# A graph transformer layer: three heads for each squaring instruction, from three PSUM banks, in place of two heads from two

## The chip, the cores and the metric

The kernel runs on one core of a Trainium2 chip. The metric is the device time of one execution in microseconds (us). Before the change it is 252.06 us, the median of three runs (251.73 to 252.9).

## The reference, cut to what matters

A layer over 625 nodes of 256 features: layer norm, then a graph step (mean of the neighbours' rows, two linear maps) and an attention step side by side, both added to x; then layer norm, and a feed forward net of 1024 hidden units whose output projection is that of one of eight experts for each node. The part that matters here is the attention, with 8 heads of 32 dimensions. Its weights are a second order expansion of exp, so that it has no maximum and no exponential:

```python
qn = _normalize(q) * (scale * temperature)
kn = _normalize(k) * scale
vN = v1 / N                      # v1 is v with a column of ones ahead
kv_mod = jnp.einsum('bhni,bhnj,bhne->bhije', kn, kn, vN)
kv = jnp.einsum('bhnd,bhne->bhde', kn, vN)
vsum = jnp.sum(vN, axis=-2)[:, :, None, :]
y = A * jnp.einsum('bhni,bhnj,bhije->bhne', qn, qn, kv_mod) \
    + scale ** 2 * Bc * jnp.einsum('bhnd,bhde->bhne', qn, kv) + scale ** 4 * Cc * vsum
y = y[..., 1:] / y[..., :1]      # A = 0.5, Bc = Cc = 1
```

For one query and one key with the product s the weight is s*s/2 + c*s + c*c (c is a constant). The kernel computes it as the square of (s + c) plus c*c, up to a factor that the division removes: so each score is computed once, squared with a bias, and multiplied by v.

## The kernel before, in words

All five engines run programs written out by hand, with semaphores between them; nothing is planned by a compiler. The order of the work on an engine is the order of its source. In order of time: the layer norm and the projections; the neighbour counts, built as products of one-hot rows (up to about 92 us of the profile); **the attention (93.6 to 126.9 us)**; transposes of the count matrix (L1146); the projections and the sum over neighbours (L1165 to L1176); the first layer of the feed forward net, its gate, the sorting of nodes by expert, the first layer again on sorted rows (L1260), the experts (L1276).

The attention computes, for a group hg of four heads (two groups), one half hf of the queries (313 or 312 of them) and one tile m of 125 keys (five tiles), two products for each head h:

- the scores (`scores`, L1085 to L1100): keys by queries, a matmul with 32 rows of the array (tile_position `(D * h, 0)`) and 125 columns, into a PSUM bank of its own;
- the values (`values`, L1103 to L1121): the squares times v, a matmul with all 125 rows and 32 columns of the array (tile_position `(0, D * h)`), accumulated over the five tiles m into 32 partitions of bank 6 or 7.

That makes 2 x 2 x 5 x 4 = 80 heads' worth of work, written as 160 matmul instructions at each of the two lines, since an fp32 product is issued as two instructions. Between the two products ScalarE squares: the source has 40 `units` (L386), each with two heads, whose scores lie in two neighbouring banks and are squared by one instruction (L622, 125 partitions x 626 elements) into one of `NGB = 4` buffers of `gsq`. `gsq` lies in `qk_sb`, where the rows of q and k were. Three pairs of banks, 0 to 5, go round (`SLOTS = 3`).

TensorE's program takes four heads at a time (two units, the index u2): `scores(u2 + 1)`, then `values(u2)`, twenty times. Its waits: `scores` waits, before each pair of heads, until the unit that used this pair of banks three units earlier is squared (L1094); `values` waits until both of its units are squared (L1107). ScalarE waits for the scores of its unit (L618) and, from the fifth unit on, until the buffer of squares is read (L620). VectorE leads each finished half out of bank 6 or 7 (L820, L823). Ahead of the loop TensorE waits until the banks of the neighbour counts are copied out by ScalarE (banks 0 and 2, L613) and VectorE (the others, L801), and fills the wait with `kept_busy` matmuls on zeros (L1083). Once, at u2 == 2, it adds up v (L1136).

Of the kernel before, what the change touches and what calls it, by code (L numbers as in the profile page):

```python
# [11 lines left out]
ACT = mybir.ActivationFunctionType  # L12
AX = mybir.AxisListType

P = 128
# [4 lines left out]
def gps_layer(nc, x, edges, w_qkv, b_qk, b_v, w_lr, b_r, w_proj, b_proj, temp,  # L20
              w1, b1, wg, bg, wd, bd, rows_sorted, out):
    N, C = out.shape
    TP = 125
    T = N // TP
# [8 lines left out]
    D = C // H  # L33
    HG = P // D
# [5 lines left out]
    HALF = [(0, (N + 1) // 2), ((N + 1) // 2, N)]  # L40
    HW = HALF[0][1]
# [7 lines left out]
    with ExitStack() as ctx:  # L49
# [6 lines left out]
        ps = ctx.enter_context(nc.psum_tensor("ps", [P, 8, BANK], F32))  # L56
# [30 lines left out]
        big = mem[:, WD:WD + BIG]  # L87
# [5 lines left out]
        sc2_col = sb("sc2_col", [P, 1])  # L93
# [22 lines left out]
        qk_sb = sb("qk_sb", [P, T * 4 * QB])  # L116
# [8 lines left out]
        qT = qkT[:, 0:2 * N].rearrange("p (k n) -> p k n", k=2)  # L125
        kT = qkT[:, 2 * N:4 * N].rearrange("p (k n) -> p k n", k=2)
# [22 lines left out]
        v = vz[:, :, 0:C]  # L149
# [6 lines left out]
        bd_all = vz_flat[:, 0:E * C]  # L156
        v_sum = row[:, 0, 0:C]
        NGB = 4
        gsq = qk_sb[0:TP, 0:NGB * 2 * HW].rearrange("p (b i n) -> p b i n", b=NGB, i=2)
        yT_sb = sb("yT_sb", [P, T * 2 * (P + 1)])  # L160
        yT = yT_sb[:, 0:2 * N].rearrange("p (k n) -> p k n", k=2)
        uq = yT
# [85 lines left out]
        A_copied_a = sem("A_copied_a")  # L248
        A_copied_v = sem("A_copied_v")
# [23 lines left out]
        s_ps = sem("s_ps")  # L273
        g_ready = sem("g_ready")
        g_used = sem("g_used")
# [38 lines left out]
        ACT_SUMS = (0, 2)  # L314
# [68 lines left out]
        FIRST_PARTS = ((0, KH // 2), (KH // 2, KH - 1), (KH - 1, KH))  # L383


        units = [(hg, hf, m, pr) for hg in range(2) for hf in range(2) for m in range(T) for pr in range(2)]  # L386
        SLOTS = 3
        LN_PARTS = ((0, 2), (2, T))

        block = ctx.enter_context(nc.Block())  # L390
# [124 lines left out]
        def _(act):  # L515
# [27 lines left out]
            for k in range(1, T):  # L543
                ins = nc.scalar.activation(ge[:, k - 1].rearrange("p g j -> p (g j)"), dst_f[:, :], ACT.Sign,
                                           bias=below[:, k - 1:k], scale=2.0)
# [57 lines left out]
            for j, (hg, hf) in enumerate(halves):  # L603
                lo, hi = HALF[hf]
# [7 lines left out]
                if n in ACT_SUMS:  # L612
                    nc.scalar.copy(sums, banks).then_inc(A_copied_a, 1)  # L613

            for u, (hg, hf, m, pr) in enumerate(units):
                lo, hi = HALF[hf]
                w = hi - lo
                act.wait_ge(s_ps, u + 1)  # L618
                if u >= NGB:
                    act.wait_ge(g_used, (u - NGB) // 2 + 1)  # L620
                b = 2 * (u % SLOTS)
                nc.scalar.activation(gsq[:, u % NGB, :, 0:w], ps[0:TP, b:b + 2, 0:w], ACT.Square,  # L622
                                     bias=sc2_col[0:TP, :]).then_inc(g_ready, 1)

            for n, (counts, blocks) in enumerate(at_parts()):
                if n in ACT_AT:
# [20 lines left out]
            for part in range(2):  # L647
                lo, hi = columns(part)
# [25 lines left out]
        def _(dve):  # L674
# [106 lines left out]
            for hg in range(2):  # L781
                nc.vector.tensor_tensor(MA[:, hg, :], ps[:, 7, QB * hg:QB * hg + P], blk[:, :], ALU.mult)
                ins = nc.vector.tensor_scalar(ks[:, hg:hg + 1], ps[:, 7, QB * hg + P:QB * (hg + 1)], 2 * SC2, None,
                                              ALU.mult)
# [4 lines left out]
            for j, (hg, hf) in enumerate(halves):  # L789
                lo, hi = HALF[hf]  # L790
# [25 lines left out]
            dve.wait_ge(v_sum_read, 1)  # L816
            for k in range(4):
                hg, (lo, hi) = k // 2, HALF[k % 2]
                dve.wait_ge(g_used, T * (k + 1))
                nc.vector.scalar_tensor_tensor(yT[:, hg, lo:hi], ps[:, 6 + k % 2, 0:hi - lo], vs[:, hg:hg + 1],  # L820
                                               rn[:, hg, lo:hi], ALU.add, ALU.mult).then_inc(y_left, 1)
                dve.wait_ge(y_left, k + 1)
                nc.vector.tensor_scalar(yT[:, hg, lo:hi], yT[:, hg, lo:hi], bv_sb[:, hg:hg + 1], None, ALU.add  # L823
                                        ).then_inc(y_ready, 1)
                if k == 0:
                    step(nc.vector.reciprocal(rn[:, 1, :], rn[:, 1, :]))
# [7 lines left out]
            for t in range(T):  # L834
                a, rest = (ps[0:TP, b, :] for b in RP_BANKS[t % 2])
# [24 lines left out]
            for part, tiles in enumerate(TOKENS):  # L860
                lo, hi = columns(part)
                own, NT = slice(tiles[0], tiles[-1] + 1), len(tiles)
# [79 lines left out]
        def _(pe):  # L942
            mm = nc.tensor.matmul
# [122 lines left out]
            for j, (hg, hf) in enumerate(halves):  # L1066
                lo, hi = HALF[hf]
# [3 lines left out]
            for j, (hg, hf) in enumerate(halves):  # L1071
                lo, hi = HALF[hf]
# [8 lines left out]
            def kept_busy(n, b):  # L1081
                for _ in range(n):
                    mm(ps[:, b, :], zeros[:, 0:P], zeros[:, :], start=True, stop=True)  # L1083

            def scores(u2):  # L1085
                hg, hf, m, _ = units[2 * u2]
                lo, hi = HALF[hf]
                for h in range(HG):
                    u = 2 * u2 + h // 2
                    if h % 2 == 0 and u < SLOTS:  # L1090
                        pe.wait_ge(A_copied_a, (1, 2, 2)[u])
                        pe.wait_ge(A_copied_v, (1, 2, 4)[u])
                    if h % 2 == 0 and u >= SLOTS:
                        pe.wait_ge(g_ready, u + 1 - SLOTS)  # L1094
                    rows = slice(D * h, D * (h + 1))
                    ins = mm(ps[0:TP, 2 * ((2 * u2 + h // 2) % SLOTS) + h % 2, 0:hi - lo],  # L1096
                             kT[rows, hg, TP * m:TP * (m + 1)], qT[rows, hg, lo:hi], start=True, stop=True,
                             tile_position=(D * h, 0))
                    if h % 2:
                        ins.then_inc(s_ps, 1)  # L1100


            def values(u2):  # L1103
                hg, hf, m, _ = units[2 * u2]
                lo, hi = HALF[hf]
                k = 2 * hg + hf
                pe.wait_ge(g_ready, 2 * u2 + 2)  # L1107
                if u2 == 0:
                    pe.wait_ge(A_copied_v, 5)
                if k == 1 and m == 0:  # L1110
                    pe.wait_ge(v_sum_read, 1)
                if m == 0 and k >= 2:
                    pe.wait_ge(y_left, k - 1)
                for pr in range(2):
                    for i in range(2):
                        h = 2 * pr + i
                        ins = mm(ps[D * h:D * (h + 1), 6 + k % 2, 0:hi - lo],  # L1117
                                 v[:, m, P * hg + D * h:P * hg + D * (h + 1)],
                                 gsq[:, (2 * u2 + pr) % NGB, i, 0:hi - lo], start=(m == 0), stop=(m == T - 1),
                                 tile_position=(0, D * h), skip_group_check=True)  # L1120
                ins.then_inc(g_used, 1)  # L1121

            U2 = len(units) // 2
            pe.wait_ge(b7_free, JOBS)
            kept_busy(3, 7)
            scores(0)
            kept_busy(2, 7)
            for u2 in range(U2):
                if u2 + 1 < U2:
                    scores(u2 + 1)  # L1130
                if u2 == 0:
                    kept_busy(2, 7)
                if u2 == 2:
                    pe.wait_ge(v_tiles, 1)
                    for hg in range(2):
                        ins = mm(ps[:, 7, C + hg:C + hg + 1], v_sum[:, P * hg:P * (hg + 1)], ones_c[0:TP, 0:1],  # L1136
                                 start=True, stop=True)
                    ins.then_inc(v_sum_ps, 1)
                values(u2)

            pe.wait_ge(g_ready, len(units))
            pe.wait_ge(A_ready, T)
# [183 lines left out]
```

## Time and profile before

| | |
|---|---|
| median of three runs | 252.06 us |
| the profiled execution | 251.73 us |
| its span, first to last instruction | 250.0 us |
| mean granted TensorE clock | 0.997 of full speed |
| TensorE matmuls busy | 235.7 us, 94% of the span |
| VectorE busy | 148.2 us, 59% |
| ScalarE busy | 145.2 us, 58% |
| attention, first scores to first transpose | 93.6 to 126.9 us |

All times come from one profiled execution. A busy share is an average over stages with different limits; the chain of waits says which engine set the time of a stretch. Matmuls that run at the same time in different parts of the array are shown as one merged row with a count ("x8"), whose second number is the length from the first start to the last end.

### The profile page before, as it was taken

The numbers are of one execution on the slowest core, as the hardware profiler recorded it, in microseconds if no ns is written. First come the engines' busy times: TensorE is split into PE (matmuls) and PEld (weight loads), VectorE is DVE, ScalarE is ACT, GpSimd is POOL, SyncE is SP. The second block draws the span as 40 slices with busy tenths as digits, with TensorE's granted clock in tenths as the row PEclk, the third lists the DMA queues.
The fourth block names the chain that finished last, engine by engine and source line by source line (L and its number), as shares of the span: only waits on it lengthen the run. The fifth ranks groups of instructions, "written<-read, shape, count | busy, mean of one in ns | idle before, by whom it ended". The sixth has DMA issues, their size and how long they took to land.

```text
span 250.0 us, 4726 instructions
## 1 busy us (share of the span) xinstructions
PE 235.7 (94%) x1428; PEld 149.4 (60%) x1429; DVE 148.2 (59%) x422; ACT 145.2 (58%) x223; POOL 31.7 (13%) x64
## 2 busy tenths in 40 slices
PE   7899999999897999999999999998899999999990
PEld 2448676655454553433378886564455578888880
DVE  2999999999999969950134649523700243223320
ACT  3977998999999967899950116443043332333000
POOL 7460000000000019100000000000540000000331
PEclk9999999999999999999999999999999999999998
DMA  6560000000000000199910000030123000000111
GB/s 233 194 215 3 1 3 5 3 4 5 0 5 3 3 3 3 37 413 425 416 59 4 0 0 0 24 134 9 32 79 106 0 1 3 0 1 3 38 34 33
DMA packets 6030, 15.82 MB, mean 63 GB/s; under 512 B 2724, under 2 KB 3783, under 8 KB 4723
## 3 DMA queue, kind: packets, MB, share of 16 engines
q1 hardware_dynamic: 4432, 12.64, 13.6%
q0 software_dynamic: 1280, 1.31, 2.0%
q10 hardware_dynamic: 288, 1.44, 1.4%
q8 instruction: 21, 0.34, 0.6%
q14 instruction: 9, 0.07, 0.1%
HBM read 14.08 MB, written 1.30 MB: 62 GB/s over the span
## 4 chain that ended last, share of the span: by engine, by line
PE 69%; DVE 26%; ACT 1%; issue 1%; POOL 1%; DVEq 0%; POOLq 0%
PE ps L1276 17%; DVE mem L728 14%; PE ps L1214 7%; PE ps L1096 7%; PE ps L1260 6%; DVE mem L731 6%; PE ps L1117 5%; PE ps L1176 4%; PE ps L1010 4%; PE ps L1244 3%; PE ps L945 3%; PE ps L1165 2%; PE ps L1167 2%; PE ps L973 1%; DVE qk_sb L774 1%
## 5 line engine op out<-in xcount | busy, mean ns | idle before, releaser
L523 ACT ACTIVATE mem<-ids_m,half_src 125x628 bf16<-125x628 f16 x96 | 69.8, 815 | 0.0
L1010 PE MATMUL ps<-mem 125*128 125x501 bf16 x180 | 51.3, 374 | 2.2 <-issue 2.0
L728 DVE TENSOR_SCALAR mem<-node_ids,dst_f 125x628 bf16<-125x628 f16 x160 | 52.1, 371 | 0.0
L1276 PE MATMUL ps<-mem 128*125 x192 | 41.6, 379 | 0.0
L1012 PE MATMUL ps<-mem 125*128 125x126 bf16 x180 | 39.3, 219 | 0.0
L1276 PEld LDWEIGHTS ps<-mem 128*125 128x125 f32 x192 | 36.0, 188 | 5.4
L1010 PEld LDWEIGHTS ps<-mem 125*128 x180 | 17.6, 98 | 22.5 <-issue 4.8
L622 ACT ACTIVATE qk_sb<-ps,sc_col 125x626 f32<-125x626 f32 (+1 forms) x40 | 28.6, 779 | 3.7 <-PE ps L1096 3.7
L731 DVE TENSOR_SCALAR mem<-ids_m,src_f 125x628 bf16<-125x628 f16 x64 | 23.9, 374 | 0.0
L671 ACT COPY mem<-mem 128x1000 f32 x8 | 8.2, 1031 | 19.8 <-PE ps L1276 19.8
L1096 PE MATMUL ps<-mem 32*125 32x313 f32 (+1 forms) x160 | 19.1, 472 | 0.2 <-DVE mem L801 0.2
L1012 PEld LDWEIGHTS ps<-mem 125*128 x180 | 17.5, 97 | 2.3 <-issue 1.2
L1214 PE MATMUL ps<-xnT,w_sb 128*128 128x375 f32 (+1 forms) x64 | 18.4, 432 | 0.0
L935 DVE SCALAR_TENSOR_TENSOR row<-vz,row x12 | 5.8, 485 | 20.1 <-issue 20.1
L920 DVE COPY mem<-mem 128x500 f32 (+2 forms) x12 | 4.1, 393 | 20.3 <-ACT mem L663 20.0
L505 POOL DMA_INDIRECT rows_sorted<-row,pos x5 | 6.2, 1236 | 77.3 <-DVE pos L893 76.1
L1260 PE MATMUL ps<-xnT,w_sb 128*128 128x512 f32 (+1 forms) x56 | 15.3, 433 | 0.0
L1117 PE MATMUL ps<-qk_sb,vz 125*32 125x313 f32 (+1 forms) x160 | 14.7, 439 | 0.6 <-ACT qk_sb L622 0.6
L1096 PEld LDWEIGHTS ps<-mem 32*125 32x125 f32 x160 | 8.9, 180 | 10.5 <-issue 5.0
L1214 PEld LDWEIGHTS ps<-xnT,w_sb 128*128 128x128 f32 x64 | 11.6, 189 | 5.5 <-ACT mem L651 1.2
L973 PE MATMUL ps<-wqkv_sb,xnT 128*125 128x512 f32 (+1 forms) x40 | 14.1, 487 | 0.8 <-ACT xnT L551 0.8
L651 ACT ACTIVATE mem<-ps,b_sb 128x375 f32<-128x375 f32 (+1 forms) x16 | 8.3, 522 | 9.4 <-PE ps L1214 9.4
(204 smaller groups left out, 280.0 us busy)
## 6 DMA issues: line engine op xcount, KB each, us to landing
mem<-in_wd SPq DMA_DIRECT2D x8, 1024.0 KB, 13.1
w_sb<-in_w SPq DMA_DIRECT2D x1, 1024.0 KB, 8.2
vz<-in_bd SPq DMA_DIRECT2D x1, 1000.0 KB
wqkv_sb<-in_w_qkv ACTq DMA_DIRECT2D x1, 768.0 KB, 6.1
x_all<-in_x ACTq DMA_DIRECT2D x1, 640.0 KB, 4.7
row<-rows_sorted SPq DMA_DIRECT2D x1, 579.7 KB
wlr_sb<-in_w_lr SPq DMA_DIRECT2D x1, 512.0 KB, 5.5
bqk_all<-in_b_qk SPq DMA_DIRECT2D x1, 256.0 KB, 4.7
```

What stands on the lines that cost most here:

```text
L523: ins = nc.scalar.activation(oh[:, g % OHB, 0, j, :], ids_m1[:, :], ACT.Sign, bias=half_src[:, g * GC + j:g * GC + j + 1])
L622: nc.scalar.activation(gsq[:, u % NGB, :, 0:w], ps[0:TP, b:b + 2, 0:w], ACT.Square, bias=sc2_col[0:TP, :]).then_inc(g_ready, 1)
L728: ins = nc.vector.tensor_scalar(oh[:, g % OHB, 1, j, :], node_ids[:, :], dst_f[:, col:col + 1], None, ALU.is_equal)
L731: ins = nc.vector.tensor_scalar(oh[:, g % OHB, 0, j, :], ids_m1[:, :], src_f[:, col:col + 1], 2.0, ALU.is_ge, ALU.mult)
L973: ins = mm(ps[0:TP, QKV_BANKS[n], lo:hi], xnT[:, c, TP * t:TP * (t + 1)], w[:, c, :], start=(c == 0), stop=(c == KC - 1))
L1010: mm(psf[:, bass.ds(tile * BANK, TW + 1)], node_of, oh[:, buf, 0, j, 0:TW + 1], start=False, stop=False, skip_group_check=True)
L1012: mm(psf[:, bass.ds(tile * P + 5 * BANK, AW)], node_of, oh[:, buf, 0, j, TW:N + 1], start=False, stop=False, skip_group_check=True)
L1096: ins = mm(ps[0:TP, 2 * ((2 * u2 + h // 2) % SLOTS) + h % 2, 0:hi - lo], kT[rows, hg, TP * m:TP * (m + 1)], qT[rows, hg, lo:hi], start=Tru ...
L1117: ins = mm(ps[D * h:D * (h + 1), 6 + k % 2, 0:hi - lo], v[:, m, P * hg + D * h:P * hg + D * (h + 1)], gsq[:, (2 * u2 + pr) % NGB, i, 0:hi ...
L1214: ins = mm(fa_bank(part, k), w1_sb[:, c, P * k:P * (k + 1)], x2nT[:, c, lo:hi], start=(c == 0), stop=(c == KC - 1))
L1260: ins = mm(psf[:, at + lo:at + hi], w1_sb[:, c, P * k:P * (k + 1)], x2nT[:, c, lo:hi], start=(c == 0), stop=(c == KC - 1))
L1276: ins = mm(ps[0:TP, 4 + n % EB, 0:C], hT_step[:, n % EB, k, :], wd_sb[:, bass.ds(e, 1), k, :], start=(k == 0), stop=(k == KH - 1))
```

## The change

A unit now holds up to three heads (`UH = 3`). For each of the four combinations of group and half, the 20 pairs (m, h) are listed in order and cut into 6 units of three and one of two: 28 units in all instead of 40, each squared by one instruction from up to three neighbouring banks. There are two slots of three banks (0 to 2, 3 to 5). TensorE's loop goes over units instead of pairs of units: `scores(u + 2)`, then `values(u)`, 28 times, with one more `scores(1)` ahead of it. A unit may hold heads of two key tiles. `scores` waits once, ahead of its first head, for the unit two earlier; `values` waits for its own unit. The buffers of squares are four of 3 x 313 elements, in `big` (where the one-hot rows of the counts were), instead of four of 2 x 313 in `qk_sb`. The wait for the count banks is put ahead of each head of the first two units.

```diff
@@ -156,7 +156,8 @@
         bd_all = vz_flat[:, 0:E * C]
         v_sum = row[:, 0, 0:C]
         NGB = 4
-        gsq = qk_sb[0:TP, 0:NGB * 2 * HW].rearrange("p (b i n) -> p b i n", b=NGB, i=2)
+        UH = 3
+        gsq = big[0:TP, 0:NGB * UH * HW].rearrange("p (b i n) -> p b i n", b=NGB, i=UH)
         yT_sb = sb("yT_sb", [P, T * 2 * (P + 1)])
         yT = yT_sb[:, 0:2 * N].rearrange("p (k n) -> p k n", k=2)
         uq = yT
@@ -383,8 +384,10 @@
         FIRST_PARTS = ((0, KH // 2), (KH // 2, KH - 1), (KH - 1, KH))
 
 
-        units = [(hg, hf, m, pr) for hg in range(2) for hf in range(2) for m in range(T) for pr in range(2)]
-        SLOTS = 3
+        heads = [(m, h) for m in range(T) for h in range(HG)]
+        units = [(k, heads[n:n + UH]) for k in range(4) for n in range(0, len(heads), UH)]
+        PER_K = len(units) // 4
+        SLOTS = 2
         LN_PARTS = ((0, 2), (2, T))
 
         block = ctx.enter_context(nc.Block())
@@ -612,15 +615,14 @@
                 if n in ACT_SUMS:
                     nc.scalar.copy(sums, banks).then_inc(A_copied_a, 1)
 
-            for u, (hg, hf, m, pr) in enumerate(units):
-                lo, hi = HALF[hf]
-                w = hi - lo
+            for u, (k, own) in enumerate(units):
+                lo, hi = HALF[k % 2]
                 act.wait_ge(s_ps, u + 1)
                 if u >= NGB:
-                    act.wait_ge(g_used, (u - NGB) // 2 + 1)
-                b = 2 * (u % SLOTS)
-                nc.scalar.activation(gsq[:, u % NGB, :, 0:w], ps[0:TP, b:b + 2, 0:w], ACT.Square,
-                                     bias=sc2_col[0:TP, :]).then_inc(g_ready, 1)
+                    act.wait_ge(g_used, u - NGB + 1)
+                b = UH * (u % SLOTS)
+                nc.scalar.activation(gsq[:, u % NGB, 0:len(own), 0:hi - lo], ps[0:TP, b:b + len(own), 0:hi - lo],
+                                     ACT.Square, bias=sc2_col[0:TP, :]).then_inc(g_ready, 1)
 
             for n, (counts, blocks) in enumerate(at_parts()):
                 if n in ACT_AT:
@@ -816,7 +818,7 @@
             dve.wait_ge(v_sum_read, 1)
             for k in range(4):
                 hg, (lo, hi) = k // 2, HALF[k % 2]
-                dve.wait_ge(g_used, T * (k + 1))
+                dve.wait_ge(g_used, PER_K * (k + 1))
                 nc.vector.scalar_tensor_tensor(yT[:, hg, lo:hi], ps[:, 6 + k % 2, 0:hi - lo], vs[:, hg:hg + 1],
                                                rn[:, hg, lo:hi], ALU.add, ALU.mult).then_inc(y_left, 1)
                 dve.wait_ge(y_left, k + 1)
@@ -1082,61 +1084,58 @@
                 for _ in range(n):
                     mm(ps[:, b, :], zeros[:, 0:P], zeros[:, :], start=True, stop=True)
 
-            def scores(u2):
-                hg, hf, m, _ = units[2 * u2]
-                lo, hi = HALF[hf]
-                for h in range(HG):
-                    u = 2 * u2 + h // 2
-                    if h % 2 == 0 and u < SLOTS:
-                        pe.wait_ge(A_copied_a, (1, 2, 2)[u])
-                        pe.wait_ge(A_copied_v, (1, 2, 4)[u])
-                    if h % 2 == 0 and u >= SLOTS:
-                        pe.wait_ge(g_ready, u + 1 - SLOTS)
+            def bank_left(b):
+                if b in ACT_SUMS:
+                    pe.wait_ge(A_copied_a, 1 + ACT_SUMS.index(b))
+                else:
+                    pe.wait_ge(A_copied_v, b + 1 - sum(a < b for a in ACT_SUMS))
+
+            def scores(u):
+                k, own = units[u]
+                hg, (lo, hi) = k // 2, HALF[k % 2]
+                if u >= SLOTS:
+                    pe.wait_ge(g_ready, u + 1 - SLOTS)
+                for i, (m, h) in enumerate(own):
+                    b = UH * (u % SLOTS) + i
+                    if u < SLOTS:
+                        bank_left(b)
                     rows = slice(D * h, D * (h + 1))
-                    ins = mm(ps[0:TP, 2 * ((2 * u2 + h // 2) % SLOTS) + h % 2, 0:hi - lo],
-                             kT[rows, hg, TP * m:TP * (m + 1)], qT[rows, hg, lo:hi], start=True, stop=True,
-                             tile_position=(D * h, 0))
-                    if h % 2:
-                        ins.then_inc(s_ps, 1)
-
-
-            def values(u2):
-                hg, hf, m, _ = units[2 * u2]
-                lo, hi = HALF[hf]
-                k = 2 * hg + hf
-                pe.wait_ge(g_ready, 2 * u2 + 2)
-                if u2 == 0:
-                    pe.wait_ge(A_copied_v, 5)
-                if k == 1 and m == 0:
+                    ins = mm(ps[0:TP, b, 0:hi - lo], kT[rows, hg, TP * m:TP * (m + 1)], qT[rows, hg, lo:hi],
+                             start=True, stop=True, tile_position=(D * h, 0))
+                ins.then_inc(s_ps, 1)
+
+            def values(u):
+                k, own = units[u]
+                hg, (lo, hi) = k // 2, HALF[k % 2]
+                pe.wait_ge(g_ready, u + 1)
+                if u == 0:
+                    bank_left(6)
+                if u == PER_K:
                     pe.wait_ge(v_sum_read, 1)
-                if m == 0 and k >= 2:
+                if u % PER_K == 0 and k >= 2:
                     pe.wait_ge(y_left, k - 1)
-                for pr in range(2):
-                    for i in range(2):
-                        h = 2 * pr + i
-                        ins = mm(ps[D * h:D * (h + 1), 6 + k % 2, 0:hi - lo],
-                                 v[:, m, P * hg + D * h:P * hg + D * (h + 1)],
-                                 gsq[:, (2 * u2 + pr) % NGB, i, 0:hi - lo], start=(m == 0), stop=(m == T - 1),
-                                 tile_position=(0, D * h), skip_group_check=True)
+                for i, (m, h) in enumerate(own):
+                    ins = mm(ps[D * h:D * (h + 1), 6 + k % 2, 0:hi - lo], v[:, m, P * hg + D * h:P * hg + D * (h + 1)],
+                             gsq[:, u % NGB, i, 0:hi - lo], start=(m == 0), stop=(m == T - 1),
+                             tile_position=(0, D * h), skip_group_check=True)
                 ins.then_inc(g_used, 1)
 
-            U2 = len(units) // 2
             pe.wait_ge(b7_free, JOBS)
             kept_busy(3, 7)
             scores(0)
             kept_busy(2, 7)
-            for u2 in range(U2):
-                if u2 + 1 < U2:
-                    scores(u2 + 1)
-                if u2 == 0:
-                    kept_busy(2, 7)
-                if u2 == 2:
+            scores(1)
+            kept_busy(2, 7)
+            for u in range(len(units)):
+                if u + SLOTS < len(units):
+                    scores(u + SLOTS)
+                if u == 3:
                     pe.wait_ge(v_tiles, 1)
                     for hg in range(2):
                         ins = mm(ps[:, 7, C + hg:C + hg + 1], v_sum[:, P * hg:P * (hg + 1)], ones_c[0:TP, 0:1],
                                  start=True, stop=True)
                     ins.then_inc(v_sum_ps, 1)
-                values(u2)
+                values(u)
 
             pe.wait_ge(g_ready, len(units))
             pe.wait_ge(A_ready, T)
```

## Rows read from the trace of the kernel before

**Rows 1.** The page: busy time of each engine; the chain that ended last.
```profile
PE 235.7 (94%) x1428; PEld 149.4 (60%) x1429; DVE 148.2 (59%) x422; ACT 145.2 (58%) x223; POOL 31.7 (13%) x64
...
PE 69%; DVE 26%; ACT 1%; issue 1%; POOL 1%; DVEq 0%; POOLq 0%
```

**Rows 2.** The chain in order of time: start us, us, what; the attention's start, middle, end.
```profile
94.96 0.54 PE ps L1083 x2
...
109.56 0.66 PE ps L1117 x8
110.22 0.74 PE ps L1096 x8
110.96 0.67 PE ps L1117 x8
111.63 1.00 PE ps L1096 x6
...
126.89 2.92 PE ps L1146 x25
```

**Rows 3.** Groups of instructions by form, 93 to 128 us: busy, mean ns; idle before.
```profile
L622 ACT ACTIVATE qk_sb<-ps,sc_col 125x626 f32<-125x626 f32 x20 | 14.4, 779 | 2.9 <-PE ps L1096 2.9
L622 ACT ACTIVATE qk_sb<-ps,sc_col 125x624 f32<-125x624 f32 x20 | 14.3, 778 | 0.8 <-PE ps L1096 0.8
```

**Rows 4.** Timeline 90 to 104 us, other engines and the sum of v.
```profile
92.75 1.06 ACT L613 COPY mem<-ps 125x501 f32<-125x501 f32 x2 [1.95 <-PE ps L1077]
92.75 2.63 DVE L801 COPY mem<-ps 125x501 f32<-125x501 f32 x5 [2.20 <-PE ps L1077]
94.41 1.46 ACT L622 ACTIVATE qk_sb<-ps,sc_col 125x626 f32<-125x626 f32 x2 [0.60 <-PE ps L1096]
96.70 0.73 PE L1117 MATMUL ps<-qk_sb,vz 125*32 125x313 f32 x8
...
99.77 0.60 PE L1136 MATMUL ps<-ones_c,row 125*128 125x1 f32 x4
100.30 0.16 PEld L1117 LDWEIGHTS ps<-qk_sb,vz 125*32 125x32 f32 x8
```

**Rows 5.** Timeline of narrow windows in the middle: start us, us, instructions merged.
```profile
110.15 0.54 PE L1096 MATMUL ps<-mem 32*125 32x313 f32 x4
...
110.52 0.44 PE L1096 MATMUL ps<-mem 32*125 32x313 f32 x4
110.89 0.73 PE L1117 MATMUL ps<-qk_sb,vz 125*32 125x312 f32 x8
111.56 1.07 PE L1096 MATMUL ps<-mem 32*125 32x313 f32 x8
112.55 0.73 PE L1117 MATMUL ps<-qk_sb,vz 125*32 125x313 f32 x8
```

**Rows 6.** Timeline of narrow windows at the start, TensorE: two heads by themselves.
```profile
93.58 0.53 PE L1096 MATMUL ps<-mem 32*125 32x313 f32 x2 [0.20 <-DVE mem L801]
...
93.92 0.46 PE L1096 MATMUL ps<-mem 32*125 32x313 f32 x2
...
94.17 0.53 PE L1096 MATMUL ps<-mem 32*125 32x313 f32 x2
...
94.50 0.46 PE L1096 MATMUL ps<-mem 32*125 32x313 f32 x2
94.89 0.60 PE L1083 MATMUL ps<-zeros 125*128 125x512 bf16 x2
95.43 0.81 PE L1096 MATMUL ps<-mem 32*125 32x313 f32 x8
96.17 0.60 PE L1083 MATMUL ps<-zeros 125*128 125x512 bf16 x2
```

**Rows 7.** Groups of ScalarE over the span, by form: activations from PSUM of three sizes.
```profile
L663 ACT ACTIVATE mem<-ps,b_sb 128x625 f32<-128x625 f32 x8 | 6.3, 782 | 9.9 <-PE ps L1260 9.7 <-PE ps L1255 0.2
L651 ACT ACTIVATE mem<-ps,b_sb 128x375 f32<-128x375 f32 x8 | 4.5, 574 | 4.1 <-PE ps L1214 4.1
L651 ACT ACTIVATE mem<-ps,b_sb 128x250 f32<-128x250 f32 x8 | 3.8, 470 | 5.3 <-PE ps L1214 5.3
```

**Rows 8.** Timeline 121 to 129 us: the end of the attention.
```profile
124.80 0.73 PE L1117 MATMUL ps<-qk_sb,vz 125*32 125x312 f32 x8
126.15 0.73 PE L1117 MATMUL ps<-qk_sb,vz 125*32 125x312 f32 x8 [0.61 <-ACT qk_sb L622]
126.81 2.37 PEld L1146 LDWEIGHTS ps<-ident,at_sb 125*125 125x125 f32 x21 [0.51 <-issue]
```

## The prediction, written before the change was run

> **What bounds the kernel now.** I read the page first: TensorE is busy 94% of the span, ScalarE 58%, and 69% of the chain that ended last is TensorE's [rows 1]. For the attention this average says little, so I read the chain there in order of time. Without a break it consists of score blocks (L1096) and value blocks (L1117) of TensorE, in a pattern of four that repeats: 0.66, 0.74, 0.67, 1.00 us [rows 2]. That is 3.07 us for two steps of four heads, about 1.53 us each. The groups by form show the other side: 40 squarings of 779 and 778 ns, busy for 28.7 us together, with 3.7 us idle, all of it waiting for TensorE's scores [rows 3]. Two squarings without a wait last 1.46 us [rows 4], so the second starts 1.46 - 0.78 = 0.68 us after the first: ScalarE needs 4 x 0.68 = 2.72 us of each 3.07. So both engines are nearly full, and the reader should ask what each would need alone.
>
> TensorE alone: the timeline of the middle shows a score block from 110.15 and the value block behind it from 110.89, then the next scores at 111.56: 0.74 + 0.67, taken together 1.40 [rows 5]. The block that starts at 111.56 takes until 112.55, 0.99 us: the row of the chain is the long one. There the second pair of heads had to wait for ScalarE. So ScalarE costs TensorE some 0.26 us in every second step, and TensorE alone would need 2.80 of the 3.07 us. This is all that a better ScalarE side can give back: 0.13 us a step, 20 steps, 2.7 us.
>
> **What a block costs.** In rows 5 the first instructions of four heads start together at 110.15, the second ones together at 110.52, and the next block 0.37 us later. A block is thus two waves, and the heads in a wave run side by side, each in its own 32 rows of the array. The question for this change is what a wave with three heads costs. The trace has waves with two: at 93.58 a pair starts, its second wave at 93.92, and the next pair (which waited for a bank) at 94.17, with its second wave at 94.50; the next block of another kind starts at 94.89 [rows 6]. That is 0.34 us from wave to wave, and 94.89 - 94.17 = 0.72 us for a score block of only two heads, against 0.74 with four (95.43 to 96.17, the same neighbour behind it [rows 6]). A wave costs what one head costs; two more heads add 0.02 us. A three-head score block is therefore worth 0.73 us, not three quarters of 0.74. Value blocks with fewer than four heads do not occur; they are waves in the same way (0.67 us with four, [rows 5]), and I take 0.66 for three. Its bounds are 0.50 (in proportion to the heads) and 0.67; I take the upper side, since the score blocks went that way. One step is then 0.73 + 0.66 = 1.39 us.
>
> The Trainium skill has a rule here (TensorE: Matmul & The Clock Gate, section "Why this matters for your kernels"): heads in distinct row groups run concurrently, four tiles reach 3.07 times one tile's rate, three tiles in column groups 2.38 times. An estimate from these two figures: a wave of three costs (3/2.38)/(4/3.07) = 0.97 of a wave of four, so a step costs 0.97 x 1.40 = 1.36 instead of 1.39 and the time would be 0.8 us less than the sum below. The trace's pair (0.72 against 0.74) gives the same 0.97 for two heads already.
>
> **The change, part by part.**
>
> *Fewer, longer squarings.* 24 of 939 elements and 4 of 626. From 375 to 625 elements an activation from PSUM grows from 574 to 782 ns and from 250 to 375 by 104 ns, 0.83 ns per element both times [rows 7]. So 313 more elements make 0.78 + 0.26 = 1.04 us, one each 0.94 us where they follow without a wait. ScalarE's need falls from 40 x 0.68 = 27.2 to 24 x 0.94 + 4 x 0.68 = 25.3 us: 1.9 us, off the path as soon as TensorE needs more. A third bank might cost extra in one instruction; nothing here shows it. The bound is at what point it would matter: scores that start at T have their second wave at T + 0.36, and in the first unit squaring began 94.41 - 93.95 = 0.46 us behind a second wave that started by 93.95 (the pair's second instruction lies 0.03 behind the 93.92 of the row [rows 4, 6]); that makes T + 0.84, squared at T + 1.88, seen by TensorE by T + 1.93. The scores two steps later need it, at T + 2.78. The squaring may be 0.85 us longer before it costs anything.
>
> *28 steps instead of 20.* This is the price. Each step has one score block and one value block, with a change of the array's shape on either side, and three heads in it where there were four (in four of the steps two). The steps' sum grows from 20 x 1.53 = 30.6 to 28 x 1.39 = 38.9 us. Nothing hides it: TensorE is the chain.
>
> *One wait instead of two in a score block.* The wait in mid-block goes with its 0.26 us; it is already in the 1.40. What is late next is TensorE itself.
>
> *The start.* Scores of the first unit need banks 0, 1, 2. ScalarE's second copy (bank 2) ends at 92.75 + 1.06 = 93.81 [rows 4]; the third head starts some 0.15 us later, as the pair did behind VectorE's copy, at 93.96, its second wave at 94.30, the squaring at 94.76 (94.41 before), done at 95.80. Behind the scores two zero matmuls (0.54 from 94.65 [rows 2]); the second unit's scores at 95.19, whose third head needs bank 5: VectorE's five copies end at 92.75 + 2.63 = 95.38, the fourth about 0.2 before, so it starts near 95.34 and the block ends at 96.06; two more zero matmuls, and the loop's first scores start at 96.60. The squares of unit 0 are long there.
>
> *The loop.* Step n starts at 96.60 + 1.39 n, plus 0.53 once for the sum of v (99.77 to 100.30 [rows 4]). Step 25, the last with scores: 96.60 + 34.75 + 0.53 = 131.88. Its scores 0.73: 132.61. Then three value blocks in a row, without scores between them. With the shape unchanged each should take two waves of 0.29 (half of 0.67 less the change of about 0.09), 0.57: 133.18, 133.75, and 134.40 with the change behind the last. The transposes, which started at 126.81 [rows 8], start at 134.40: 7.6 us later.
>
> *The other edits* cost nothing: `gsq` in other memory leaves all instructions as long as they were; its wait counts (four buffers, read one unit at a time) are met two steps ahead; VectorE's four exits at L820 follow TensorE as before, and only the last lies behind the last value block, hidden by 2.92 us of transposes [rows 2] as now. All later work hangs on TensorE's order and moves with it. The loads of the experts' weights, which run under the attention, are not waited for at its end.
>
> **Sum.** 251.73 (the profiled execution: 250.0 of span and 1.7 around it) + 7.6 = 259.3. The median of the runs shown lies 0.3 above the profiled one; I say **259.4 us**.
>
> **The rivals.**
> - *Heads, not waves, set TensorE's price* (the other side). If a block costs in proportion to its heads, a step is 3/4 of 1.40 = 1.05 us. Against the sum: 25 x 0.34 = 8.5 and 0.6 in the last blocks less: 259.4 - 9.1 = 250.3, faster by 1.8. It would decide wherever a step costs less than about 1.39 - 7.6/27 = 1.11 us. For it: only that value blocks with fewer heads are nowhere to be seen. Against: the two-head score blocks [rows 6]. Chance 0.04.
> - *ScalarE is the bound and the change relieves it.* The squarings then run without a gap: from 97.44 (third unit's scores at 96.60 + 0.84) another 25.3 - 1.9 = 23.4 to 120.9, values and change 0.7: 121.6, 5.2 before 126.8, so 246.5. The gaps in ScalarE's row speak for it only in part (3.7 us idle are TensorE's doing [rows 3]). The Trainium skill (TensorEngine Tiling, section "PSUM Bottleneck") says that tiling speeds up TensorE but not the reading of PSUM, which may become the bottleneck, and that one should vectorise PSUM access. The trace does not bear that out here. Chance 0.01.
> - *Part of both*: value blocks in proportion (0.50), score blocks as waves. A step 1.23: 25 x 0.16 + 0.4 = 4.4 less, 255.0. Chance 0.04.
> - *The handshake gets longer*: two slots instead of three. If a three-bank squaring takes over 1.88 us, or the scores wait in mid-block again, a step gains the 0.26 us of the long block: 28 x 0.26 = 7.3, 266.7. Chance 0.03.
> - *The clock*: it is 0.997 on average; TensorE's gaps get shorter, not longer. At half speed the stage would last tens of us more. Chance 0.01.
>
> **How the numbers follow.** The forecast's own case has 0.87: its range, from steps of 1.36 to 1.42 (25 x 0.03 = 0.8) and 0.6 for the runs' scatter, is 258.0 to 260.9; as it holds over 8 in 10, that is the range, with 0.2 more below for value blocks of three that are slightly cheaper: 257.8 to 260.9. A change under 0.5% (1.3 us) can't be told from none. Faster by more: the first two rivals, 0.05. Within: a step between 1.06 and 1.16 us, 0.02. Slower: the rest, 0.93.
>
> **What would show it.** In the changed kernel: the chain of the attention still all TensorE, with blocks near 0.73 (L1096's new line) and 0.66 us, x6 each, none of 1.00; 28 squarings, most near 1.04 us, with gaps of 0.4 us between them; the transposes near 134.4. It is wrong if value or score blocks are near 0.5 us, or if ScalarE's row has no gaps.

## The result: slower by 2.8%

The changed kernel takes 259.31 us (median; 258.94 to 259.31, four runs) against 252.11 us (251.73 to 252.9, four runs, one more than above): a ratio of 1.028, 95% interval 1.026 to 1.030. The forecast was 259.4, the range 257.8 to 260.9. The profiled span is 257.6 us against 250.0.

The page of the changed kernel, busy times and the chain that ended last, answers to [rows 1]:

```profile
PE 243.4 (94%) x1428; PEld 150.4 (58%) x1429; DVE 148.6 (58%) x422; ACT 144.7 (56%) x211; POOL 31.7 (12%) x64
...
PE 66%; DVE 27%; ACT 2%; DMA 2%; issue 1%; POOL 0%; DVEq 0%; ACTq 0%
```

TensorE has the same 1428 matmuls and is busy 7.7 us longer; ScalarE has 12 instructions fewer and is busy 0.5 us less. Neither share of the span says which of the two set the time.

The chain of the changed kernel in order of time (start us, us, what), the middle and the end of the attention, answers to [rows 2]; L1103 are the scores, L1118 the values, L1145 the transposes:

```profile
109.38 0.66 PE ps L1118 x6
110.03 0.73 PE ps L1103 x6
110.76 0.66 PE ps L1118 x6
111.42 0.73 PE ps L1103 x6
112.15 0.66 PE ps L1118 x6
...
132.18 0.72 PE ps L1103 x4
132.90 1.60 PE ps L1118 x16
134.50 2.59 PE ps L1145 x22
```

The long blocks of 1.00 us are gone, as the change means them to be. But the blocks, now with three heads (x6, two instructions a head), last 0.73 and 0.66 us, practically what they lasted with four (0.74 and 0.67, [rows 2]). From 109.38 to 112.15 two steps take 2.77 us, 1.385 each, for three heads a step, six in all; before, two steps took 3.07 us for eight heads.

ScalarE's side, groups by form from 93 to 136 us (count, busy, mean ns, idle before), answers to [rows 3]:

```profile
L624 ACT ACTIVATE mem<-ps,sc_col 125x939 f32<-125x939 f32 x12 | 12.5, 1044 | 4.8 <-PE ps L1103 4.8
L624 ACT ACTIVATE mem<-ps,sc_col 125x936 f32<-125x936 f32 x12 | 12.5, 1042 | 4.7 <-PE ps L1103 4.7
```

A squaring of three banks lasts 1.04 us, as worked out; ScalarE now idles 9.5 us in all ahead of these 24, 0.34 us ahead of most. It was relieved, and nobody needed it. The timeline of the changed kernel shows the same (start, length, idle before):

```profile
109.96 0.80 PE L1103 MATMUL ps<-mem 32*125 32x312 f32 x6
...
110.82 1.04 ACT L624 ACTIVATE mem<-ps,sc_col 125x936 f32<-125x936 f32 x1 [0.34 <-PE ps L1103]
...
112.20 1.04 ACT L624 ACTIVATE mem<-ps,sc_col 125x936 f32<-125x936 f32 x1 [0.34 <-PE ps L1103]
112.73 0.29 PEld L1103 LDWEIGHTS ps<-mem 32*125 32x125 f32 x4 [0.51 <-issue]
```

The scores of a unit start at 109.96, its squaring at 110.82, and the squares are ready at 111.86. The scores that use its banks next start at 112.73, 0.87 us later. The prediction's 0.85 us had 0.05 for the hand-over taken off already, so the number to set beside it is 0.82.

### The profile page after: what moved, and what is told of

Same layout as the page of the kernel before. It is cut to its first block, busy times and chain, and to the rows that moved or that the text cites. A ratio compares the mean times of both kernels' runs of the same rounds, so it can differ in the third digit from the quotient of the medians.

```text
span 257.6 us, 4699 instructions
## 1 busy us (share of the span) xinstructions
PE 243.4 (94%) x1428; PEld 150.4 (58%) x1429; DVE 148.6 (58%) x422; ACT 144.7 (56%) x211; POOL 31.7 (12%) x64
## 3 DMA queue, kind: packets, MB, share of 16 engines
q0 software_dynamic: 1280, 1.31, 1.9%
## 4 chain that ended last, share of the span: by engine, by line
PE 66%; DVE 27%; ACT 2%; DMA 2%; issue 1%; POOL 0%; DVEq 0%; ACTq 0%
PE ps L1275 16%; DVE mem L730 14%; PE ps L1103 8%; PE ps L1118 7%; PE ps L1213 7%; PE ps L1259 6%; DVE mem L733 6%; PE ps L1175 4%; PE ps L1012 4%; PE ps L1243 3%; DMA edges_sb<-in_edges 2%; PE ps L1164 2%; PE ps L1166 2%; DVE qk_sb L776 1%; PE ps L1145 1%
## 5 line engine op out<-in xcount | busy, mean ns | idle before, releaser
L730 DVE TENSOR_SCALAR mem<-node_ids,dst_f 125x628 bf16<-125x628 f16 x160 | 53.1, 387 | 0.0
L624 ACT ACTIVATE mem<-ps,sc_col 125x939 f32<-125x939 f32 (+3 forms) x28 | 28.2, 1006 | 11.3 <-PE ps L1103 11.3
L733 DVE TENSOR_SCALAR mem<-ids_m,src_f 125x628 bf16<-125x628 f16 x64 | 25.0, 390 | 0.0
L1103 PE MATMUL ps<-mem 32*125 32x313 f32 (+1 forms) x160 | 22.9, 472 | 0.0
L1118 PE MATMUL ps<-mem,vz 125*32 125x313 f32 (+1 forms) x160 | 19.8, 438 | 0.0
L1103 PEld LDWEIGHTS ps<-mem 32*125 32x125 f32 x160 | 8.9, 180 | 14.1 <-issue 13.0
L822 DVE SCALAR_TENSOR_TENSOR yT_sb<-ps,vs,mem 128x313 f32<-128x313 f32 (+1 forms) x4 | 2.2, 544 | 23.1 <-PE ps L1118 23.1
```

The source lines that it names most:

```text
L624: nc.scalar.activation(gsq[:, u % NGB, 0:len(own), 0:hi - lo], ps[0:TP, b:b + len(own), 0:hi - lo], ACT.Square, bias=sc2_col[0:TP, :]).the ...
L730: ins = nc.vector.tensor_scalar(oh[:, g % OHB, 1, j, :], node_ids[:, :], dst_f[:, col:col + 1], None, ALU.is_equal)
L733: ins = nc.vector.tensor_scalar(oh[:, g % OHB, 0, j, :], ids_m1[:, :], src_f[:, col:col + 1], 2.0, ALU.is_ge, ALU.mult)
L1103: ins = mm(ps[0:TP, b, 0:hi - lo], kT[rows, hg, TP * m:TP * (m + 1)], qT[rows, hg, lo:hi], start=True, stop=True, tile_position=(D * h, 0))
L1118: ins = mm(ps[D * h:D * (h + 1), 6 + k % 2, 0:hi - lo], v[:, m, P * hg + D * h:P * hg + D * (h + 1)], gsq[:, u % NGB, i, 0:hi - lo], start ...
```

## The experiments

Theory A: a block costs TensorE two waves whatever number of heads is in it, so 28 steps instead of 20 are the loss. Theory B: a block costs in proportion to its heads, and the loss comes from something else in the change (longer squarings, two slots, the new place of the squares).

**Smaller units.** `UH = 2` and `UH = 1` in the changed kernel:

```diff
-        UH = 3
+        UH = 2        # the second run: UH = 1
```

> The changed kernel with units of two heads (UH = 2): 40 steps instead of 28, each with half as many heads as the four of the kernel before; ScalarE squares 40 times 626 elements, as before the change. Theory A (a block costs two waves, whatever number of heads is in it): a step costs 0.72 + 0.65 = 1.37 us, 12 more steps cost 16.4 us, 24 steps lose a head and 0.014 us each: 259.3 + 16.4 - 0.3 = 275.4 us. Theory B (a block costs in proportion to its heads; the changed kernel is slower by something else, its longer squarings or its two slots): the steps' sum stays, 259 us, or less, since squarings and slots are those of smaller units.

> The changed kernel with units of one head (UH = 1): 80 steps. Theory A: 52 more steps than 28, at about 1.36 us each, 70.7 us: 259.3 + 70.7 - 0.6 = 329.4 us; score blocks near 0.71 us, value blocks near 0.64. Theory B (in proportion to the heads): 259 us. A straight line of the times against 28, 40 and 80 steps would give the price of a step by its slope.

Two heads: 275.03 us (two runs; ratio to before 1.091, 1.084 to 1.098), where theory A said 275.4. One head: 328.15 us (two runs; 1.302, 1.294 to 1.310), where it said 329.4. The work in heads is the same in all three, and so is their number of matmuls. Per added step the time grows by (275.03 - 259.31)/12 = 1.31 us and (328.15 - 275.03)/40 = 1.33 us, a little under a step's length. The steps that were there already get slightly shorter, and the start and the end do too: in the chains, from the first scores to those of the loop it is 3.19 us with three heads, 2.69 with two and 2.58 with one, and from the end of the last scores to the transposes 1.60, 1.58 and 1.32. The chain of the kernel with two heads shows the step:

```profile
113.50 0.72 PE ps L1103 x4
114.23 0.65 PE ps L1118 x4
...
119.00 0.45 PE ps L1103
```

And the chain of the kernel with one head:

```profile
113.17 0.72 PE ps L1103 x2
113.89 0.64 PE ps L1118 x2
...
118.61 0.45 PE ps L1103
```

From 113.50 to 119.00 are four steps of 1.375 us, from 113.17 to 118.61 four of 1.360. A step with one head costs 1.360, with two 1.375, with three 1.385, with four 1.400 (below): each head more adds about 0.013 us to 1.35. Theory B, which gives 259 for both, is out.

**The third head left out.** The order of work, the waits and the squarings stay:

```diff
-                for i, (m, h) in enumerate(own):
+                for i, (m, h) in enumerate(own[:2]):   # in scores and in values
```

(In the first two units the waits for the count banks are all put ahead of the first head.)

> The changed kernel, 28 steps and 28 squarings of up to 939 elements as they are, but TensorE computes scores and values only for the first two heads of each unit; the third's are left out (24 of 80 heads' work on TensorE). Theory A (waves): a step loses 0.014 us, 24 of them 0.3 us: 259.0 us. Theory B (proportion to heads): blocks lose a third, 24 x 0.46 = 11 us, ScalarE's 0.94 per step becomes the bound: about 249 us.

258.98 us (1.027 of before, 1.022 to 1.032). Measured beside it, the changed kernel with single squarings (next) took 259.0. Taking 24 of 80 heads off TensorE is worth a few tenths of a us at most: its chain, below, has blocks of 0.72 and 0.65 us, x4, where the changed kernel has 0.73 and 0.66, x6.

```profile
113.56 0.65 PE ps L1119 x4
114.20 0.72 PE ps L1104 x4
114.93 0.65 PE ps L1119 x4
```

**Each head squared by itself**, in the changed kernel:

```diff
-                nc.scalar.activation(gsq[:, u % NGB, 0:len(own), 0:hi - lo], ps[0:TP, b:b + len(own), 0:hi - lo],
-                                     ACT.Square, bias=sc2_col[0:TP, :]).then_inc(g_ready, 1)
+                for i in range(len(own)):
+                    ins = nc.scalar.activation(gsq[:, u % NGB, i, 0:hi - lo], ps[0:TP, b + i, 0:hi - lo],
+                                               ACT.Square, bias=sc2_col[0:TP, :])
+                ins.then_inc(g_ready, 1)
```

> The changed kernel, but each unit is squared by one instruction per head (3 x 313 elements, 80 instructions) instead of one for three banks. ScalarE then needs 3 x 0.43 = 1.29 us per step instead of 0.94. Theory A (TensorE's steps of 1.385 us are the bound, ScalarE has slack: squares are ready 0.84 + 0.43 + 0.43 + 0.52 = 2.22 us after the scores' start and wanted at 2.77): 259.3 us, at most 0.2 more at the very end, where the last value block waits for the last squares. Theory B (the length of the squaring sets the step, so that merging three heads in one instruction gained something): 24 x 0.35 = 8 us slower, 268 us.

259.0 us (1.027, 1.022 to 1.032), the same as the changed kernel within the scatter. In the chain, from the first scores to the transposes, it is 40.82 us against 40.66: 0.16 more, nearly all behind the last scores (1.75 us instead of 1.60), as theory A allows for. So the title's part of the change, three heads in one squaring, is worth at most that once TensorE's steps are what they are. In its timeline four squarings from 114.43 on take 1.91 us. Three of them are one unit; less the fourth's own length (estimated above at 0.52) they take 1.39, a whole step. ScalarE has no gap between these units, and TensorE's blocks of 0.73 and 0.66 us (from 113.57 and 114.30) do not move.

```profile
113.57 0.80 PE L1105 MATMUL ps<-mem 32*125 32x313 f32 x6
...
114.30 0.73 PE L1120 MATMUL ps<-mem,vz 125*32 125x312 f32 x6
114.43 1.91 ACT L625 ACTIVATE mem<-ps,sc_col 125x313 f32<-125x313 f32 x4 [0.46 <-PE ps L1105]
```

**The squares moved, alone**, in the kernel before:

```diff
-        gsq = qk_sb[0:TP, 0:NGB * 2 * HW].rearrange("p (b i n) -> p b i n", b=NGB, i=2)
+        gsq = big[0:TP, 0:NGB * 2 * HW].rearrange("p (b i n) -> p b i n", b=NGB, i=2)
```

> The kernel before with one part of the change alone: the four buffers of squares (2 x 313 elements each) lie in the memory of the one-hot rows instead of where q and k were. All theories: 252.1 us, no change (ScalarE's squarings 0.78 us, value blocks 0.66 us). If the place of the squares had a part in the loss, up to 7 us more.

251.8 us, ratio 1.000 (0.998 to 1.001). The place has no part in it.

**What the mid-block wait is.** The kernel before, squares moved, half of the columns squared:

```diff
-                nc.scalar.activation(gsq[:, u % NGB, :, 0:w], ps[0:TP, b:b + 2, 0:w], ACT.Square,
+                nc.scalar.activation(gsq[:, u % NGB, :, 0:w // 2], ps[0:TP, b:b + 2, 0:w // 2], ACT.Square,
```

> The kernel before (squares moved as in the run beside it), but ScalarE squares only the first half of the columns of each bank (2 x 156 elements); the other half of the squares is left out. It asks what a faster ScalarE side can give at most. Theory A: the wait in mid-block (0.26 us in every second step) comes from the time between the start of a score block and its first squared pair, 0.84 + 0.78 + 0.05 = 1.67 us against a step of 1.40; with 0.52 for the squaring it is 1.41 and the wait goes: steps of 1.40, 20 x 0.13 = 2.7 us less, and 0.6 us at the end, where the last value block waits for two squarings: 248.8 us, no score block near 1.00 us. Theory B (TensorE could go faster than 1.40 a step once ScalarE no longer holds it): below 246 us.

249.62 us (0.991, 0.990 to 0.993). The chain has no score block near 1.00 us any more, and none under the 0.73 us of four heads either:

```profile
113.81 0.74 PE ps L1096 x8
114.55 0.66 PE ps L1117 x8
115.21 0.74 PE ps L1096 x8
115.95 0.66 PE ps L1117 x8
...
118.01 0.74 PE ps L1096 x8
```

From 113.81 to 118.01 three steps take 4.20 us, 1.400 each: TensorE's own pace with four heads. The most that any relief on ScalarE's side can bring this kernel is thus 2 to 3 us. The 248.8 expected was too low by 0.8. It counted ten long blocks, 2.7 us; the chain of the kernel before has eight, 8 x 0.26 = 2.1. At the end, where the last value block waits for the last squares in both kernels, it gains 0.52 us (from the end of the last scores to this block 1.53 us before, 1.01 now). Together, from the first scores to the transposes, 33.31 us become 30.76. The medians (251.76 and 249.62) differ by 2.1, 0.4 less; in this kernel's profiled run the copies of the count banks began 0.36 us later (93.11 against 92.75), in a part that the edit does not touch.

**A first version with VectorE's help.** From step 9 on, in the kernel before (ScalarE squares only the other three heads of a step, and waits of TensorE for VectorE's heads are added in the same way):

```diff
+            def second_squared(u):
+                lo, hi = HALF[units[u][1]]
+                dve.wait_ge(s_ps, u + 1)
+                dve.wait_ge(g_used, (u - NGB) // 2 + 1)
+                own = gsq[:, u % NGB, 1, 0:hi - lo]
+                nc.vector.tensor_scalar(own, ps[0:TP, 2 * (u % SLOTS) + 1, 0:hi - lo], SC2, None, ALU.add
+                                        ).then_inc(gv_left, 1)
+                dve.wait_ge(gv_left, helps(u))
+                nc.vector.tensor_tensor(own, own, own, ALU.mult).then_inc(gv_ready, 1)
```

> A version meant to beat both: the kernel before, with its blocks of four heads, but from step 9 on VectorE (idle there) takes the second head of each step: it adds the constant on the way out of the bank (313 elements), which frees the bank, then squares in place; ScalarE squares the first head alone and the last two together. The first pair's banks are then free 0.84 + 0.52 + 0.05 = 1.41 us after the block's start instead of 1.67, and the mid-block wait should go in 11 steps: 11 x 0.13 = 1.4 us and up to 0.3 at the end: 250.5 us. If the wait were due to something else, or if VectorE's two instructions and its exits came too late: 252 us or more.

251.49 us against 251.76 (0.9985, 0.9976 to 0.9994): 0.3 us less by the medians and 0.4 by the ratio, where 1.4 to 1.7 were expected. The chain around the second exit tells where the rest went:

```profile
111.85 0.79 PE ps L1124 x8
112.64 0.66 PE ps L1147 x8
113.30 1.12 PE ps L1124 x8
114.42 0.66 PE ps L1147 x8
115.09 0.74 PE ps L1124 x8
```

The blocks are 0.74 and 0.79, but for one of 1.12 (and a second at 120.80, behind the third exit): VectorE's two exit instructions (0.54 and 0.38 us from 112.14) stood ahead of the second head that was due at 112.62, and it started at 113.01 (timeline of this version). The two blocks cost 2 x 0.38 = 0.76 us. And from step 9 on there were only four long blocks to shorten, 1.0 us, not the 1.4 of the expectation:

```profile
112.14 0.54 DVE L846 SCALAR_TENSOR_TENSOR yT_sb<-ps,vs,mem 128x312 f32<-128x312 f32 x1
...
112.62 1.20 ACT L632 ACTIVATE qk_sb<-ps,sc_col 125x313 f32<-125x313 f32 x2 [0.20 <-PE ps L1124]
112.71 0.38 DVE L849 TENSOR_SCALAR yT_sb<-yT_sb,bv_sb 128x312 f32<-128x312 f32 x1
113.01 0.48 DVE L832 TENSOR_SCALAR qk_sb<-ps 125x313 f32<-125x313 f32 x1
```

**The filler, and a version that beats both.** The kernel before without the second filler of its start, and the same with VectorE's other work dealt out step by step:

```diff
-                if u2 == 0:
-                    kept_busy(2, 7)
```

```diff
+            led_out(0)
+            beside = {6: (bias_added, 0), 7: (inverted, 0), 8: (inverted, 1), 9: (inverted, 2), 10: (led_out, 1),
+                      11: (bias_added, 1), 12: (inverted, 3), 13: (inverted, 4), 14: (inverted, 5), 15: (led_out, 2),
+                      16: (bias_added, 2), 17: (inverted, 6), 18: (inverted, 7)}
+            for j in range(FROM, len(units) // 2):       # FROM = 6
+                second_squared(2 * j)
+                if j in beside:
...
```

> The kernel before without the two zero matmuls that stand between the second score block and the first value block. In the trace of before they take 0.54 us (from 96.17 to 96.70), and nothing is waited for there: the first two pairs are squared at 95.87, the last count bank is copied out at 95.39, both before 96.17. Theory A (pure filler on the path): 0.54 us less, give or take 0.13 by where the mid-block waits of 0.26 us fall: 251.8 - 0.5 = 251.3 us. Theory B (they keep the granted clock up, or hide a wait): no gain, or several us more with a lower clock in the stretch behind them.

> The kernel before, without that filler and with VectorE taking the second head of each step from step 6 on; VectorE's other work in this stretch (the two instructions that lead a finished half out, and the second reciprocal, cut in ten pieces) is dealt out one instruction per step behind its squares, where the first version with VectorE's help had two long blocks (1.12 us) just where a finished half was led out. Theory A: in 14 steps the mid-block wait falls from 0.26 in every second block to 0.06: 7 x 0.20 = 1.4 us less, and 0.5 of the filler: 251.8 - 1.9 = 249.9 us. Theory B (VectorE's own load, near 1.4 us per step, becomes the bound): blocks of 0.8 to 1.0 us remain, 251 us.

Without the filler: 251.53 us against 252.12 (0.9973, 0.9956 to 0.9989), 0.6 us less where 0.5 were expected (0.48 in the chain, from the first scores to the transposes); no clock was lost (the granted clock is 1.00 in all stretches of the attention). The chain of this kernel:

```profile
113.13 0.80 PE ps L1096 x8
113.94 0.66 PE ps L1117 x8
114.60 0.93 PE ps L1096 x8
```

The waits are now spread over both score blocks, 0.80 and 0.93 instead of 0.74 and 1.00, with the same sum to 0.01. With both: **250.14 us** (0.9929, 0.9916 to 0.9943; 249.9 expected), 2.0 us faster than the kernel before (1.4 to 2.1 by the interval) and about 9 faster than the changed one. In the chain it is 1.66 us less from the first scores to the transposes (31.65 against 33.31). From 106.94 on the score blocks of this last version alternate between 0.74 and 0.79 to 0.80 where [rows 2] alternated between 0.74 and 1.00:

```profile
106.94 0.73 PE ps L1142 x8
107.68 0.66 PE ps L1165 x8
108.34 0.80 PE ps L1142 x8
109.14 0.66 PE ps L1165 x8
109.80 0.74 PE ps L1142 x8
```

## Why the prediction was right, point by point

- **The price of a wave** was the step on which all else rests, and it was read from the two-head blocks of [rows 6]. The runs with one, two and three heads show it directly: 1.360, 1.375, 1.385 us a step, and the run with the third head left out shows it at an unchanged order of work.
- **Three-head value blocks**, taken at 0.66 from bounds of 0.50 and 0.67 without a row of their own, are 0.66. The estimate weighed there from the Trainium skill (TensorE: Matmul & The Clock Gate, "Why this matters for your kernels"), 1.36 us a step, was too low by 0.025 us, as the trace has 1.385.
- **ScalarE's 1.04 us** for 939 elements is 1.04, and its slack of 0.85 is 0.82. The first squaring starts 0.86 us behind its scores; the prediction had 0.84, though its two terms, 0.36 and 0.46, make 0.82. The run with single squarings used about 0.35 us of this slack in each step without a change in the steps.
- **The sum was 0.4 us too large.** From the start of the copies to the transposes' weights it was 126.81 - 92.75 = 34.06 before and is 134.43 - 93.21 = 41.22: 7.2 us more, not 7.6. The start took 3.75 us (93.21 to 96.96, below) against my 3.85; a step 1.385 against 1.39, 0.1 over 25; and the last three value blocks 1.60 us in a row (132.83 to 134.43) against my 1.79 (134.40 - 132.61). There heads of neighbouring units overlap, with no scores between them: four value matmuls start together at 132.83, though a unit has three heads. This would have made it shorter still, but the last unit, whose squares are ready at 132.95 + 0.78 = 133.73, starts at 133.78. The prediction had no such wait in its end.
- **The 7.6 us in the two spans agree by chance**: the copies of the count banks began 0.46 us later in the profiled run of the changed kernel, before any of its changed work. The medians differ by 7.2. I had put the forecast 0.3 under the median of before plus 7.6, which hid the 0.4.

The timeline of the changed kernel, for the start and the end:

```profile
93.21 2.63 DVE L803 COPY mem<-ps 125x501 f32<-125x501 f32 x5 [2.30 <-PE ps L1079]
...
93.84 1.26 PE L1103 MATMUL ps<-mem 32*125 32x313 f32 x6
...
95.57 0.92 PE L1103 MATMUL ps<-mem 32*125 32x313 f32 x6
...
96.96 0.80 PE L1103 MATMUL ps<-mem 32*125 32x313 f32 x6
...
132.83 1.67 PE L1118 MATMUL ps<-mem,vz 125*32 125x312 f32 x16
132.95 0.78 ACT L624 ACTIVATE mem<-ps,sc_col 125x624 f32<-125x624 f32 x1 [0.33 <-PE ps L1103]
...
133.78 0.14 PEld L1118 LDWEIGHTS ps<-mem,vz 125*32 125x32 f32 x4 [0.28 <-ACT mem L624]
134.43 2.15 PEld L1145 LDWEIGHTS ps<-ident,at_sb 125*125 125x125 f32 x19 [0.51 <-issue]
```

And its window from 132.80 to 132.95, TensorE alone, for the four that start together:

```profile
132.83 0.47 PE L1118 MATMUL ps<-mem,vz 125*32 125x312 f32 x4
```

- **The rivals.** Proportional blocks, alone or with the values only, fell with the runs of fewer heads; ScalarE as the bound fell with the single squarings (259.0 us, though each step has about 0.35 us more for ScalarE to do). The longer handshake did not come: no block of 1.00 us. The clock is 1.00 in every stretch of the attention, of the changed kernel too.
- **Where I overrated something**: the mid-block wait was called ScalarE's cost, as if from its load, and counted for ten blocks, where the chain has eight. It is a delay, from one block's start to its first squared pair, 1.67 us against a step of 1.40. The trace of the kernel before shows this for the long block of [rows 5]:

```profile
111.00 2.86 ACT L622 ACTIVATE qk_sb<-ps,sc_col 125x626 f32<-125x626 f32 x4 [0.21 <-PE ps L1096]
```

The scores of the block ahead start at 110.15. ScalarE has been idle for 0.21 us, waiting for them, when it starts the squaring at 111.00; that one is done at 111.00 + 0.78 = 111.78, and the second pair's first scores in the block of 111.56 start at 111.84, 0.28 late. So ScalarE was not behind with its work; of its side only the length of one squaring counts. This sum also gives the other pattern: a step that follows one of 1.40 us waits 1.67 - 1.40 = 0.27, one that follows 1.46 waits 0.21, one that follows 1.59 waits 0.08, and any two steps in a row make 1.67 + 1.40 = 3.07 us. Without the filler the blocks are 0.93 and 0.80 instead of 1.00 and 0.74, which fits to 0.02. This is read from the traces; no run shortens the delay and leaves ScalarE's load as it is.

## What to carry to other kernels

Where an array runs small products side by side, count its work in waves, not in products: here a group that fills three of four places cost as much as a full one (1.385 against 1.400 us), so an instruction saved on the evacuating engine must not be paid for with more, emptier blocks. Before merging instructions on an engine that looks nearly full, look in the chain for what it really holds up (here 0.26 us in every second block), since that bounds the gain. And an engine that takes over part of the work needs its own other work cut small and dealt out between, or a single pair of instructions eats the gain.

## What the runs showed of the hardware that was not expected

The price of one more head in a block is the same small amount from one to four: 1.360, 1.375, 1.385, 1.400 us a step, about 0.013 us for four more matmuls. Value matmuls of successive units with no score block between them share a wave: at 132.83 four start together, three of one unit and one of the next. Two zero matmuls meant to keep the array busy cost their full 0.5 us and brought no clock here: it is 1.00 without them.
